# Filter units of one token parity and two filters, and TensorE's other parts moved to the odd slots

## The reference, cut to what matters

```python
def _stu_conv(phi, u, n):
    # U_plus  = causal convolution of u with each of 16 filters
    # U_minus = the same for u * (-1)^t, times (-1)^t
...
for i, frac in enumerate((1, 2, 4, 8)):
    xi = x[:, :T // frac]                       # a branch sees the first 1/frac of the tokens
    si = spectral(xi) + autoregressive(xi, M_u[i])    # sums over the 16 filters of U @ M
    ...
out = sum of the branches, each times its weight
```

## Time and profile before

| | |
|---|---|
| median of 3 runs | 13719.36 us |
| the profiled execution | 13716.28 us |
| its span | 13714.6 us |
| mean granted clock of TensorE | 0.979 |
| PE, DVE, ACT busy | 12826.0, 11719.2, 11100.2 us |
| token stage, one slice of 400 us from 10100 us: PE, DVE, ACT busy | 382.42, 351.18, 341.96 us |
| passes 3 to 15, period | 410 to 421 us |

### The profile page before, as it was taken

The page is one execution under the profiler, slowest core; times in us unless marked ns, Lnnn a source line. Parts: engine busy times, 40 slices in busy tenths (PEclk is TensorE's granted clock), DMA queues, the critical chain, the costliest instruction groups (busy, mean ns, idle before and its releaser), DMA issues. The chain is left out here.

```text
span 13714.6 us, 333279 instructions
## 1 busy us (share of the span) xinstructions
PE 12826.0 (94%) x134802; PEld 6856.0 (50%) x134802; DVE 11719.2 (85%) x21048; ACT 11100.2 (81%) x7140; POOL 251.4 (2%) x125
## 2 busy tenths in 40 slices
PE   8999999999999999999767999999999999999999
PEld 3333333343333333333323666666666666666668
DVE  8888898888888888888799888888888898888881
ACT  7878788787887878878688888888888888888871
POOL 0000000000000000000000000000000000000000
PEclk9999999999999999999989999999999999999999
DMA  0000000000000000000010111111111111111113
GB/s 11 2 6 2 6 2 2 6 2 6 2 2 6 2 6 2 2 6 2 28 34 6 45 45 47 49 47 50 43 46 48 48 48 47 44 47 48 47 52 99
DMA packets 331113, 357.83 MB, mean 26 GB/s; under 512 B 36232, under 2 KB 316688, under 8 KB 329616
## 3 DMA queue, kind: packets, MB, share of 16 engines
q1 hardware_dynamic: 329616, 335.51, 8.6%
HBM read 314.14 MB, written 21.23 MB: 24 GB/s over the span
## 5 line engine op out<-in xcount | busy, mean ns | idle before, releaser
L139 PE MATMUL c_acc<-c_ring,c_onehot 128*32 128x392 f32 x73728 | 6137.3, 496 | 235.9 <-DVE c_ring L260 160.6
L260 DVE TENSOR_SCALAR c_ring<-c_xn,c_w 128x1568 f32 x5760 | 5642.5, 1048 | 657.6 <-PE c_acc L139 651.5
L186 ACT ACTIVATE c_ring<-c_xn,c_w_neg 128x1568 f32 x3456 | 5330.2, 1605 | 990.5 <-PE c_acc L139 972.6
L881 ACT ACTIVATE t_ring<-t_ring 128x3136 f32<-128x3136 f32 (+4 forms) x2160 | 5140.9, 2402 | 552.6 <-DVE t_ring L1183 527.5
L1183 DVE TENSOR_SCALAR t_ring<-t_proj 128x784 f32<-128x784 f32 (+4 forms) x10240 | 4275.8, 488 | 652.0 <-PE t_psS L793 635.4
L139 PEld LDWEIGHTS c_acc<-c_ring,c_onehot 128*32 128x32 f32 x73728 | 2484.6, 111 | 3888.6 <-issue 3743.7
L793 PE MATMUL t_psS<-t_ring,t_vhot 128*32 128x392 f32 (+3 forms) x36864 | 2829.2, 436 | 163.4 <-ACT t_ring L881 137.5
L748 PEld LDWEIGHTS t_psC<-t_filter_work 128*128 128x128 f32 x12288 | 1835.6, 190 | 225.0 <-issue 46.2
L748 PE MATMUL t_psC<-t_filter_work 128*128 128x196 f32 (+3 forms) x12288 | 1828.3, 296 | 47.5 <-ACT t_filter_work L868 37.6
L793 PEld LDWEIGHTS t_psS<-t_ring,t_vhot 128*32 128x32 f32 x36864 | 1031.5, 111 | 1193.1 <-issue 543.1
L868 ACT ACTIVATE t_filter_work<-t_psC 128x392 f32<-128x392 f32 x1024 | 502.0, 490 | 617.7 <-PE t_psC L748 616.4
(11 more groups left out here) (212 smaller groups left out, 3369.8 us busy)
## 6 DMA issues: line engine op xcount, KB each, us to landing
t_filter_work<-in_toep_dram SPq DMA_DIRECT2D x512, 196.5 KB, 2.5
t_filter_work<-mix_scratch SPq DMA_DIRECT2D x512, 192.0 KB, 2.4
t_filter_work<-in_toep_dram SPq DMA_DIRECT2D x512, 98.5 KB, 2.3
t_filter_work<-mix_scratch SPq DMA_DIRECT2D x512, 64.0 KB, 1.9
mix_scratch<-t_filter_work SPq DMA_DIRECT2D x4, 2048.0 KB, 9.5
c_xin<-in_x_dram SPq DMA_DIRECT2D x8, 784.0 KB, 4.3
x_scratch<-c_xout SPq DMA_DIRECT2D x8, 784.0 KB, 3.4
t_proj<-x_scratch SPq DMA_DIRECT2D x16, 392.0 KB, 3.2
```

The costliest lines, as they stand in the source:

```text
L139: mm = pe.matmul(acc[32 * g:32 * g + 32, ch, 0:HALF], onehot[:, 31 - r:63 - r], ring[:, r % RING, g, ch * HALF:(ch + 1) * HALF], start=Fal ...
L186: act.activation(ring[:, r % RING, g, :].rearrange("c (i h w) -> c i h w", i=2, h=HW), xn[:, :, bass.ds(dy, HW), bass.ds(dx, HW)], ACT.Rel ...
L260: dve.tensor_scalar(ring[:, r % RING, g, :].rearrange("c (i h w) -> c i h w", i=2, h=HW), xn[:, :, bass.ds(dy, HW), bass.ds(dx, HW)], w0[: ...
L881: act.activation(ring[:, st % RINGS, 0:n], ring[:, st % RINGS, 0:n], ACT.Tanh).then_inc(th.s, 1)
```

## The change

- **Units.** A unit u = (j, par) is now one parity of two filters, 2j and 2j+1. `toep` holds pairs of filters; one matmul takes both filters' columns as a two-dimensional operand (392, 392, 272 and 16 columns for half 0; 392 and 136 for half 1). psC holds [filter, column] where it held [parity, column]. `mixin(m)` is for one filter: it reads the two parities from two neighbouring UT buffers and waits for the copies of both units of its pair. UTS is 4. There are still 64 units, 64 copies and 64 mixes.
- **Loads.** A filter load carries two filters and is issued ahead of every second mixing load.
- **Slots.** The filter units stand at 1 + 2u (before 3 + 2u), the mixes at 7 + 2m as before. All other PE parts of a full pass that stood in an even slot go to an odd one: the soft parts one slot later, the expert outputs two to a slot (55 to 67), the linear outputs two to a slot (97 to 103), norms 1 and 2 at 69 and 105 (before 71 and 107), norm 0 at 39 (38), the next image at 99, 101, 115 to 121 (98, 100, 117 to 123).
- **U.** The turn of U goes to slot 124 of the pass before, its copy to 126, into one of two U buffers.

```diff
-UTS = 3
+UTS = 4
-AT_OLD = {2: dict(fill=0, rowmax=1, exp=2, scale=3, pt=4, out=8), 3: dict(fill=2, rowmax=3, exp=4, scale=5, pt=12, out=16),
-          4: dict(fill=10, rowmax=11, exp=12, scale=13, pt=20, out=24), 5: dict(fill=18, rowmax=19, exp=20, scale=21, pt=26, out=30), 6: dict(pt=32, out=36)}
-AT_NEW = {0: dict(fill=38, rowmax=41, exp=42, scale=43, pt=44, out=48), 1: dict(fill=82, rowmax=85, exp=86, scale=87, pt=88, out=92)}
+AT_OLD = {2: dict(fill=1, rowmax=2, exp=3, scale=4, pt=5, out=9), 3: dict(fill=3, rowmax=4, exp=5, scale=6, pt=13, out=17),
+          4: dict(fill=11, rowmax=12, exp=13, scale=14, pt=21, out=25), 5: dict(fill=19, rowmax=20, exp=21, scale=22, pt=27, out=31), 6: dict(pt=33, out=37)}
+AT_NEW = {0: dict(fill=39, rowmax=42, exp=43, scale=44, pt=45, out=49), 1: dict(fill=83, rowmax=86, exp=87, scale=88, pt=89, out=93)}
 LN_AT = dict(stats=0, aggr=1, norm=3, turn=4, evac=5)
-AT_LN = [38, 71, 107]
-AT_MOE = dict(logits=44, bias_add=45, exp=46, rank=47, rank2=48, gate=49, turn=50, evac=51, bias=52, bias_used=53, y=54)
-AT_LIN = dict(q=77, zq=78, eq=79, qout=80, k=79, zk=80, ek=81, kout=82, v=81, vout=82, a=83, n=98)
-AT_STU = dict(u=0, uev=1, res=14, resev=16, conv=3, ar=[5, 71], out=[70, 1])
-MIX_LAG = 4
-AT_NEXT = dict(x=98, tok=99, ln=113, t=117, tev=118, w=121, wev=122)
+AT_LN = [39, 69, 105]
+AT_MOE = dict(logits=45, bias_add=46, exp=47, rank=48, rank2=49, gate=50, turn=51, evac=52, bias=53, bias_used=54, y=55)
+AT_LIN = dict(q=77, zq=78, eq=79, qout=80, k=79, zk=80, ek=81, kout=82, v=81, vout=82, a=83, n=97)
+AT_STU = dict(u=124, uev=126, res=15, resev=16, conv=1, mix=7, ar=[5, 71], out=[70, 1])
+AT_NEXT = dict(x=99, tok=100, ln=111, t=115, tev=116, w=119, wev=120)
...
+                def filters(j):
+                    half, n = divmod(2 * j, 2 * NK)
+                    cols = HALVES[half][0][1] + 1
+
+                    W(sp, pC, 2 * (j - FILTS) + 2, d)
+                    sp.dma_start(toep[:, j % FILTS, :, 0:cols], ai["toep"][:, n:n + 2, 0:cols]).then_inc(filt_in[j % FILTS].s, 16)
+                filters(0)
+                for m in range(4 * NK):
...
+                    if m % 2 == 0 and m + 2 < 4 * NK: filters(m // 2 + 1)
+
+                    W(sp, pZ, m - MIXES + 1, d)
+                    sp.dma_start(mixr[:, m % MIXES, m0:m1, :], mixd[n, :, m0:m1, :]).then_inc(mix_in[m % MIXES].s, 16)
+                    if m == MIXES - 1 and not no(d, 0): store(d - 1)
...
                 for i in range(14):
-                    yield AT_MOE["y"] + i
+                    yield AT_MOE["y"] + i // 2 * 2
...
                 for t in tiles:
-                    yield AT_LIN["n"] + t
+                    yield AT_LIN["n"] + t // 2 * 2
...
                 def conv(u):
-                    half, n = divmod(u, 2 * NK)
+
+                    j, par = divmod(u, 2)
+                    half, n = divmod(2 * j, 2 * NK)
                     (t0, t1), _ = HALVES[half]
-                    W(pe, filt_in[u % FILTS], 16 * (u // FILTS + 1), d)
+                    if par == 0: W(pe, filt_in[j % FILTS], 16 * (j // FILTS + 1), d)
                     W(pe, eC, u, d)
+                    out = psC[:, 0:HALF].rearrange("p (f t) -> p f t", f=2)
...
+                    for i in tiles_in:
+                        c0 = max(t0, 128 * i)
+                        ins = pe.matmul(out[:, :, c0 - t0:t1 - t0], U[:, src, i, :], toep[:, j % FILTS, :, 1 - shift + c0 - 128 * i:1 - shift + t1 - 128 * i],
+                                        start=(i == 0), stop=(i == tiles_in[-1]), skip_group_check=True)
                     ins.then_inc(pC.s, 1)
...
-                    W(pe, eC, u + 1, d)
+                    W(pe, eC, 2 * j + 2, d)
                     for s in branches:
                         lo, hi = SEG[s]
-                        ins = pe.matmul(sums2(lo, hi, t0), mixr[:, u % MIXES, s, :], UT[:, u % UTS, :].rearrange("p (a t) -> p a t", a=2)[:, :, lo - t0:hi - t0],
+                        ins = pe.matmul(sums2(lo, hi, t0), mixr[:, m % MIXES, s, :], UT[:, 2 * j % UTS:2 * j % UTS + 2, QUART * f + lo - t0:QUART * f + hi - t0],
                                         start=False, stop=(n == 2 * NK - 1), skip_group_check=True)
...
                     W(act, pC, u + 1, d)
-                    W(act, pZ, u - UTS + 1, d)
+                    W(act, pZ, u // 2 * 2 - 2, d)
                     act.activation(UT[:, u % UTS, :], psC[:, 0:HALF], ACT.Copy).then_inc(eC.s, 1)
```

More of the change, by code:

```diff
@@ L449, in token_layers @@
         out_ready = Ev("out_ready", 2); stored = Ev("stored", 16)
-        filt_in = [Ev(f"filter_in{i}", 16 * 4 * NK // FILTS) for i in range(FILTS)]
+        filt_in = [Ev(f"filter_in{i}", 16 * 2 * NK // FILTS) for i in range(FILTS)]
         mix_in = [Ev(f"mix_in{i}", 16 * 4 * NK // MIXES) for i in range(MIXES)]
@@ L521, in load_mix @@
             def load_mix(d):
-                for u in range(4 * NK):
-                    half, n = divmod(u, 2 * NK)
-                    m0, m1 = HALVES[half][1][0], HALVES[half][1][-1] + 1
[L526 to L531, removed]
+                def filters(j):
[5 more added lines that the diff above has]
+                for m in range(4 * NK):
+                    half, n = divmod(m, 2 * NK)
+                    m0, m1 = HALVES[half][1][0], HALVES[half][1][-1] + 1
+                    if m % 2 == 0 and m + 2 < 4 * NK: filters(m // 2 + 1)
+                    W(sp, pZ, m - MIXES + 1, d)
+                    sp.dma_start(mixr[:, m % MIXES, m0:m1, :], mixd[n, :, m0:m1, :]).then_inc(mix_in[m % MIXES].s, 16)
+                    if m == MIXES - 1 and not no(d, 0): store(d - 1)
             def one_pass(b, p, bb=None):
@@ L713, in after, with turn_u, spectral @@
                 ln(2)
-            def spectral(d):
-                sums2 = lambda lo, hi, t0: psZ[:, :, lo - t0:hi - t0]
[L717 to L723, removed]
+            def turn_u(d):
+                yield AT_STU["u"]
+                W(pe, eBT, 3, d)
+                for par in range(2):
+                    for i in range(4):
+                        c0 = 2 + par + 256 * i
+                        ins = pe.transpose(psB[:, 512 * par + 128 * i:512 * par + 128 * i + 128], nrmU[:, c0:c0 + 255:2], ident[:, :])
+                    ins.then_inc(pU.s, 1)
+            def spectral(d, p):
+                U = U2[:, p]
+                sums2 = lambda lo, hi, t0: psZ[:, :, lo - t0:hi - t0]
                 def turn_res():
@@ L736, in conv @@
                 def conv(u):
-                    half, n = divmod(u, 2 * NK)
+                    j, par = divmod(u, 2)
+                    half, n = divmod(2 * j, 2 * NK)
                     (t0, t1), _ = HALVES[half]
-                    W(pe, filt_in[u % FILTS], 16 * (u // FILTS + 1), d)
+                    if par == 0: W(pe, filt_in[j % FILTS], 16 * (j // FILTS + 1), d)
                     W(pe, eC, u, d)
+                    out = psC[:, 0:HALF].rearrange("p (f t) -> p f t", f=2)
                     tiles_in = [i for i in range(4) if 128 * i < t1]
[L742 to L749, removed]
+                    src = par if n < NK else 1 - par
@@ L778, in one_pass @@
                 if not no(b, NI - 1): tracks.append(next_image(b, 1 - p, b + 1))
-                if not no(b, 0): tracks.append(after(b - 1))
-                if not no(b, 0) and not no(b, 1): tracks.append(spectral(b - 2))
+                if not no(b, 0): tracks += [after(b - 1), turn_u(b - 1)]
+                if not no(b, 0) and not no(b, 1): tracks.append(spectral(b - 2, p))
                 def body(step):
@@ L802, in last @@
             def last():
-                run([soft_old(blk, NI, NI - 1, nrm2[:, 1]) for blk in range(2, 7)] + [after(NI - 1), spectral(NI - 2)], alone)
-                run([spectral(NI - 1)], alone)
+                run([soft_old(blk, NI, NI - 1, nrm2[:, 1]) for blk in range(2, 7)] + [after(NI - 1), turn_u(NI - 1), spectral(NI - 2, 0)], alone)
+                run([spectral(NI - 1, 1)], alone)
             passes(pe, lambda: run([next_image(-1, 0, 0)], alone), one_pass, last)
@@ L851, in after, with turn_u, spectral @@
                 ln(2)
[L852 removed]
+            def turn_u(d, p):
                 yield AT_STU["uev"]
                 W(act, pU, 2, d)
[L855 removed]
+                act.activation(U2[:, p], psB[:, :].rearrange("p (a b c) -> p a b c", a=2, b=4), ACT.Copy).then_inc(eU.s, 1)
+            def spectral(d):
                 def residual():
@@ L874, in one_pass @@
                 if not no(b, NI - 1): tracks.append(next_image(b, 1 - p))
-                if not no(b, 0): tracks.append(after(b - 1))
+                if not no(b, 0): tracks += [after(b - 1), turn_u(b - 1, 1 - p)]
                 if not no(b, 0) and not no(b, 1): tracks.append(spectral(b - 2))
@@ L886, in last @@
             def last():
-                run([soft(blk, NI - 1, dict(AT_OLD[blk], exp=AT_OLD[min(blk, 5)]["exp"])) for blk in range(2, 7)] + [after(NI - 1), spectral(NI - 2)], alone)
```

(1 more changed line is left out.)

23 lines of the change are left out of this document (10 added, 13 removed).

## The result

The changed kernel took 13588.13 us (median of 4 runs, 13581.22 to 13601.82), the kernel before 13714.36 on the same chip: 126 us less, ratio 0.9907 (95% interval 0.9895 to 0.9920). It is faster, as forecast, but by 126 us where I had summed 309, and the time lies above the stated range. The profiled execution of the changed kernel has a span of 13579.5 us.

A forecast was written before the change was run, and what follows sets the result against it. TensorE (PE), busy 398.5 of 416.3 us an image, was taken as the bound. Savings of 20 us an image x 14 = 280, plus 26 at the end and 3 in image 1, sum to 309: 13410 us, range 13320 to 13525.

The forecast's parts named there:

- Units: Filter units in the token stage: half-0 unit 2.23 to 1.99 us, half-1 1.18 to 1.05, saving 11.5 us an image.
- Visits: Even slots of a full pass: 42 no longer hold other parts beside scoring, 0.33 us saved each, 13.9 us an image.
- Each chain keeps its distances in slots: Moved soft, MoE and linear chains in the token stage: distances in slots stay the same; no cost counted.
- Two tasks of DVE in one slot, and norm 1 at 69: Paired expert and linear parts give DVE two tasks in the next slot; psB's double buffer still serves; no cost counted.
- The stretches: Pass split by slots, savings capped by other engines: 7.5 (112-32), 4 (32-48), 4.5 (48-64), 2 (64-96), 2 (96-112); 20 us an image.
- Copies and loads: ACT's evacuations and the filter loads: same copies, same bytes in half the transfers, loads issued early enough; zero effect.
- The closing part: Last two images' filter units, run alone at the end: savings of 0.24 and about 0.2 x 64 = 28, 26 us taken.
- ACT and DVE take over early: Rival, token stage: ACT and DVE bind sooner, about 10.5 us an image arrives, 170 in all: 13549; chance 0.16.
- Everything arrives: Rival, whole kernel: PE's full saving of 25.4 us an image shows, 387 in all: 13332; chance 0.13.
- loads in full view: Rival, filter units: weight loads do not overlap matmuls, halving them saves 73 us an image, DVE the floor: 13006; chance 0.01.
- nothing: Rival, odd slots: drains are paid inside them or waits eat the savings; 13716, within 0.2% (27 us); chance 0.03.
- the slower case: Rival, odd slots: filter units end late for ACT's evacuation, delaying the next tanh; 101 us slower, 13817; chance 0.05.

The follow-up runs named there:

- norm1_back: The changed kernel with norm 1 back at slot 71 instead of 69: 13545 us, ratio 0.9875 to the kernel before.
- both_third: The changed kernel with norm 1 at 71, mix and filter unit first in odd slots, third norm's turn at 111, next image's at 117 and 119: 13499 us.
- units_only: The changed kernel with only the new filter units and U's turn at 124, every other part at its slot of before: 13597 us, ratio 0.9910.
- filters_first: The changed kernel with mix and filter unit run first in an odd slot, ahead of parts that may wait for DVE: 13563 us, ratio 0.9888.

## Why the prediction was wrong

Its first half, what the instructions cost, held; the second, that the answers of the other engines would still be in time, did not. By its steps:

- **Units (11.5 us a pass).** Right. 1.99 and 1.01 us measured against 1.99 and 1.05, and PE busy 11.3 less with the units alone.
- **Visits (13.9 us).** Right in price, as far as the rows go: the 1.32 to 1.45 edge is gone from even slots, and two expert parts take 1.82. PE busy fell by 18.7 in the whole change, where 25.4 had been summed; the difference is work at half clock. By the clock records of the two traces PE stood at the lower level for 5.1 us a pass before and for 18.8 after (passes 8 and 9), and half of the 13.7 more is lost, an estimate: 6.9 us. 18.7 + 6.9 is 25.6. For the odd slots alone the same sum gives 9.3 + 3.4 (11.9 us at the lower level) = 12.7 against the 13.9 of the visits. The Trainium skill (TensorEngine Tiling (Array Packing), Key Properties) says that a change of tiling mode drains the array; the rows have 0.33 us for a visit beyond its work, and no run here shows how much of it is that drain.
- **"Each chain keeps its distances in slots", counted at nothing.** This is the step that failed. A distance in slots is not one in time, and an even slot is not an odd one. For the first norm, the chain on DVE takes 12.5 us (10090.05 to 10102.52) and took 13.0, and PE's four slots take 10.6 us (10088.65 to 10099.28) and took 11.2: neither has changed much. What changed is that DVE starts 1.4 us behind PE's scoring where it had started 1.7 ahead, because the mix and the filter unit no longer stand in between. I should have asked which scoring releases DVE's task and what PE still has to do from there to its question; I set the engines against each other only over stretches of 16 to 55 slots. Of the 17.0 us a pass by which 25.4 missed the 8.4 of passes 8 and 9, 10.3 are more waits (9.5 for DVE, the unnamed one with them, and 0.8 for ACT) and an estimated 6.9 the clock.
- **Two tasks of DVE in one slot, and norm 1 at 69.** I named the pairs and stopped at the psB buffers. Who is queued behind them on DVE wasn't asked: the adding of the first half at slot 70, for which PE waits at 71. This wait does come in part from PE's shorter slots (1.9 us with the units of before, 3.3 with the new ones). norm1_back prices the norm's part of it at 3.2 us a pass, 43 us in all.
- **The stretches.** 32 to 48 and 64 to 96, where I saw DVE 86 and 95% busy and took 4 and 2, lost 2.6 and 2.1; 96 to 112 lost 1.8 instead of winning 2. The stretch on which I thought ACT would bind, 112 to 32, gained 11.2 where 7.5 were taken. The busy time of a neighbour does not merely cap the gain of a stretch: within it PE waits for single answers.
- **Copies and loads, counted at nothing.** Right: a filter load, now of 393.0 KB, lands in 3.3 us instead of 2.5, and none of PE's waits is for one.
- **The clock.** Left out altogether. Behind the two waits of 3.3 us it fell, and half of the time spent there is lost: 3.62 us for a filter unit of 2.07.
- **The closing part.** 384.1 us before, 356.2 after (from the last scoring's end): 27.9 against the 26 taken. There PE is busy for 377.4 and 347.7 us of it and no other engine for over 78, and the sum of PE's instructions is nearly the time.
- **The rivals.** "ACT and DVE take over early" is nearest, at 13549, in part by luck: it had 3 us from 112 to 32, where 11.2 came, and gains where there were losses. Its reason (their total work) is only half of it. DVE is busy 89% and ACT 87% of the new pass, and both_third shows 5 us a pass to be had with the same work. "Everything arrives", "loads in full view" and "nothing" did not occur. ACT's waits for the end of a filter unit, the slower case's mechanism, fell from 47.1 to 31.0 us in two passes.

Here the passes with filters brought 105 us (from 7.5 a pass, on 14), the closing part 28, the rest of the program 2 of the span's 135.

What stays open: how much the units alone could bring. Of units_only's additional 2.9 us of rest a pass 0.9 are waits for ACT and 1.9 waits for DVE and the unnamed one, by its trace, but neither norm1_back's nor filters_first's remedy was tried on it. Nor was slot 43 put right by an order that gives DVE its lead back; filters_first only covers the wait.

## What to carry to other kernels

When one engine's work is cut in a pipeline whose parts are placed by slot, check every question that it asks of another engine: which event releases the other's task, what the first engine still has to do from there to its question, the other's busy time up to the answer, and what newly stands in that queue. Put work that waits for nobody in front of the part that waits. Price each saving alone before two are joined: here one of two correct savings was worth nothing on top of the other as it stood.

## What was unexpected of the hardware

A wait of 3.3 us on TensorE was followed by a stretch at the lower clock in which a filter unit took 3.62 us instead of 2.07, and four useless matmuls (2.85 us) put into such a wait took 1.9 us off the mean pass (the medians are 18 us apart, with overlapping intervals). A matmul over two filters' columns as a two-dimensional operand of 392 costs its columns and no more: its passes start 0.32 to 0.33 us apart (10011.37, 10011.69, 10012.02), as those of the mix did.
